# Twelve LayerNorm normalisations moved from VectorE to GpSimd in a linear-attention and ternary-FFN layer

## What is computed

```
xn  = (x - mean(x)) / sqrt(var(x) + 1e-5)          # over the last axis
q, k, v = xn @ Wq.T, xn @ Wk.T, xn @ Wv.T          # 16 heads, 16 features, 64 values
A   = tril(taylor_exp(q) @ taylor_exp(k).T)        # 1, x, x*x terms
y   = A @ v;  y = y * rsqrt(mean(y*y) + 1e-5) * g
f   = gelu(xn @ ternary(W1).T + b1) @ ternary(W2).T + b2
out = x + y @ Wo.T + f
```

## Time and profile before

| | us |
|---|---|
| median of 3 runs | 760.08 (760.06 to 760.13) |
| the profiled execution's own time | 760.95 |
| its span, slowest core (core 5) | 759.2 |
| spans of the other cores | 753.8 to 756.6 |
| PE, DVE, ACT, POOL busy | 691.8, 417.8, 243.4, 99.1 |
| mean granted TensorE clock, by core | 0.990 to 0.993 |

### The profile page before, as it was taken

One profiled execution on the slowest core, in us unless ns is written; L12 is line 12 of the kernel. 1 busy time (PEld: TensorE's weight loads), 2 busy tenths in 40 slices (PEclk: granted clock), 3 DMA queues, 4 the chain that ended last, 5 costly groups with the idle time before them and its releaser, 6 DMA issues.

```text
span 759.2 us, 11498 instructions; the slowest of 8 cores (753.8 to 759.2 us)
## 1 busy us (share of the span) xinstructions
PE 691.8 (91%) x4050; PEld 335.8 (44%) x4050; DVE 417.8 (55%) x623; ACT 243.4 (32%) x322; POOL 99.1 (13%) x131
## 2 busy tenths in 40 slices
PE   2777888877789888999999999999999999999998
PEld 1344544544445444444444444444444444444443
DVE  6667564678577566276556435351554554401653
ACT  3456666657557443222333333333100000000000
POOL 3112222224122211000000001010010000000000
PEclk9999999999999999999999999999999999999999
DMA  7974464766848624659786614533353676200883
GB/s 155 204 161 103 87 122 92 171 146 194 216 143 261 201 69 128 171 198 303 216 281 175 213 56 131 200 114 110 111 200 133 206 223 195 98 1 20 244 232 115
DMA packets 65415, 121.49 MB, mean 160 GB/s; under 512 B 22096, under 2 KB 28112, under 8 KB 65360
## 3 DMA queue, kind: packets, MB, share of 16 engines
q1 hardware_dynamic: 46752, 64.46, 28.0%
q0 software_dynamic: 18608, 56.30, 27.2%
HBM read 103.30 MB, written 16.78 MB: 158 GB/s over the span
## 4 chain that ended last, share of the span: by engine, by line
PE 81%; ACT 6%; DMA 5%; issue 4%; DVE 2%; POOL 2%; SPq 0%; ACTq 0%; DVEq 0%; POOLq 0%
PE pST L1199 8%; PE pY L1221 7%; PE pSS L1199 7%; PE pST L1221 7%; PE pW L1199 7%; PE pW L1221 7%; PE pSS L1221 7%; PE pY L1199 7%; PE pSS L977 4%; PE pW L1134 4%; PE pW L977 4%; PE pSS L1134 3%; ACT Am L922 3%; DMA xr<-x 2%; PE pSS L966 2%
## 5 line engine op out<-in xcount | busy, mean ns | idle before, releaser
L1221 PE MATMUL pY<-w2t,hT 128*128 128x512 bf16 x256 | 66.0, 379 | 0.1
L1221 PE MATMUL pST<-w2t,hT 128*128 128x512 bf16 x256 | 66.0, 379 | 0.0
L1221 PE MATMUL pSS<-w2t,hT 128*128 128x512 bf16 x256 | 66.0, 379 | 0.0
L1221 PE MATMUL pW<-w2t,hT 128*128 128x512 bf16 x256 | 66.0, 379 | 0.0
L524 POOL TENSOR_SCALAR_AFFINE_SELECT Am<-Am 128x1024 bf16<-128x1024 bf16 x32 | 35.3, 1104 | 208.4 <-ACT Am L922 208.4
L1199 PE MATMUL pST<-xnT,w1t 128*128 128x512 bf16 x272 | 61.5, 379 | 0.0
L1199 PE MATMUL pSS<-xnT,w1t 128*128 128x512 bf16 x256 | 57.9, 379 | 0.4 <-DVE consts L705 0.4
L1199 PE MATMUL pW<-xnT,w1t 128*128 128x512 bf16 x256 | 57.9, 379 | 0.0
L1199 PE MATMUL pY<-xnT,w1t 128*128 128x512 bf16 x240 | 54.2, 379 | 0.0
L719 DVE TENSOR_SCALAR w1t<-stg,consts 128x2048 bf16<-128x2048 f32 (+1 forms) x18 | 21.0, 1165 | 54.1 <-PE pY L1199 53.9
L517 POOL DMA_DIRECT2D stg<-w1r x32 | 25.1, 784 | 163.3 <-DVE w1t L722 147.5
(11 more groups left out here) (185 smaller groups left out, 1043.0 us busy)
## 6 DMA issues: line engine op xcount, KB each, us to landing
stg<-w1r POOLq DMA_DIRECT2D x32, 1024.0 KB, 7.5
stg<-w2r SPq DMA_DIRECT2D x16, 1024.0 KB, 9.0
stg<-w2r POOLq DMA_DIRECT2D x16, 1024.0 KB, 7.1
xr<-x SPq DMA_DIRECT2D x16, 512.0 KB, 5.2
res_scr<-rst SPq DMA_DIRECT2D x16, 512.0 KB, 3.2
res<-res_scr SPq DMA_DIRECT2D x32, 256.0 KB, 3.6
xs<-x SPq DMA_DIRECT2D x32, 256.0 KB, 3.9
out<-osb SPq DMA_DIRECT2D x32, 256.0 KB, 2.5
```

What stands on the lines that cost most here:

```text
L1221: return e.matmul(out_bank(n), hT[:, j, 128 * t:128 * t + 128], w2t[8 * dh + j // 4][:, j % 4, :], start=(j == 0), stop=(j == NJ - 1))
```

## The change

For tiles 4 to 15 the last step of LayerNorm, the subtraction and multiplication over 128x1024, is issued by GpSimd (`normalise`) in place of VectorE. VectorE keeps the statistics and the reciprocal (`ln_r`). In GpSimd's slot the late tile is normalised ahead of `affine_select`, and the slot's own tile behind it, ahead of the slot's DMA issues. VectorE gets two waits on `sXN`, ahead of bn_aggr and of the reciprocal, so that the statistics of tile t-2 aren't overwritten while GpSimd reads them. Tiles 0 to 3 stay as they were.

```diff
+        def normalise(t):
+            e.wait_ge(sLR, t + 1)
+            if t >= T_PE + 2:
+                unit_filled(e, ("t", t - 2))
+            e.tensor_scalar(xn_tm[:, t % 2, :], xr[:, t % 4, :],
+                            cc(C_MV + 2 * (t % 2)), cc(C_RC + t % 2),
+                            ALU.subtract, ALU.mult).then_inc(sXN, 1)
+
         for i in range(NI):
+            if i in LN_LATE:
+                normalise(LN_LATE[i])
 
             am = Am[:, i % 2, :, :]
             unit_emptied(e, ("s", i))
             e.affine_select(am, am, [[0, 8], [1, 128]], ALU.is_ge, 0.0, base=0,
                             channel_multiplier=-1).then_inc(gMK, 1)
+            if ln_tile(i) is not None:
+                normalise(ln_tile(i))
             if i < 2:
                 e.dma_start(out=wv[:, 1, 4 * i:4 * i + 4, :],
...
             e.wait_ge(sLB, 2 * t + 2)
+            if t >= T_PE + 2:
+                e.wait_ge(sXN, t - 1)
             e.bn_aggr(cc(C_MV + 2 * (t % 2), 2), cc(s6, 12)).then_inc(sLA, 1)
 
+        def ln_r(t):
+            e.wait_ge(sLS, t + 1)
+            if t >= T_PE + 2:
+                e.wait_ge(sXN, t - 1)
+            e.reciprocal(cc(C_RC + t % 2), cc(C_SD + t % 2)).then_inc(sLR, 1)
+
         def ln_b(t):
-            e.wait_ge(sLS, t + 1)
-            e.reciprocal(cc(C_RC + t % 2), cc(C_SD + t % 2)).then_inc(sLR, 1)
-            if t >= T_PE + 2:
-                unit_filled(e, ("t", t - 2))
-            elif t >= 2:
+            ln_r(t)
+            if t >= 2:
                 e.wait_ge(pT, t - 1)
...
             if i in LN_LATE:
-                ln_b(LN_LATE[i])
+                ln_r(LN_LATE[i])
...
             if ln_tile(i) is not None:
-                ln_b(ln_tile(i))
+                ln_r(ln_tile(i))
```

## The result

The changed kernel takes 774.64 us (median of 4 runs, 773.55 to 775.26), the kernel before beside it 760.11: ratio 1.0188, 95% interval 1.0176 to 1.0201, that is +14.3 us (13.4 to 15.3) on 760.11; the two medians differ by 14.5. Forecast was +2.8 us. The sign was right, the size five times too small, and the time lies outside the range. Some executions run longer whatever the kernel, with a lower granted clock on the cores of one die, and are left out of all ratios and medians here.

What follows compares the result with a forecast made beforehand. The chain lies on TensorE for 81% and VectorE for 2%, so relieving VectorE wins little. Terms -0.8 + 0.4 + 3.2 = +2.8 us on 760.08 give 762.9 us, range 760.9 to 765.6.

Steps and rivals of the forecast that it cites:

- The price of a tile on GpSimd: All twelve moved tiles: one normalisation on GpSimd takes 1.1 us, with 2.2 us as upper bound.
- Slot 3, query DMAs: Slot 3: four query DMAs wait behind tile 9's normalisation, so slot 4's scores move from 64.65 to 68.4, +3.8 us.
- Slots 1, 2 and 8, turning: Slots' own tiles: VectorE's next instruction waits for ScalarE anyway, so no gain; no cost was put on TensorE's turning.
- Slot 0, held products: Slot 0: GpSimd's mask, now later, holds VectorE's products of `features_k(0)`; +0.4 us, bounds 0 and +1.4.
- Slot 2, VectorE's gain: Slot 2: without the late tile, VectorE starts tile 8's statistics earlier and ScalarE's root follows; -0.8 us, bounds -0.8 and 0.
- rival (b): About the same time: a shorter wait ahead of slot 2's projection keeps the clock full; half gives +1.2, 761.3 us; chance 0.10.
- Slot 4: Slot 4 gives some back, with `own(5)` at 3.1 us: +3.2 us for slots 3 and 4 together, bounds +2.0 and +3.9.
- The late tiles: Tiles normalised ahead of the mask: the later mask costs nothing in slot 0, and 0 in slot 2, by 0.3 us.
- (a): Slower: a GpSimd tile takes 2.2 us, delaying query DMAs and slot 0 further; +4.9, 765.0 us; chance 0.15.
- (c): Faster: tile 9's reciprocal comes early enough that query DMAs land before slot 4's scores need them; -2.5, 757.6 us; chance 0.05.
- (d): VectorE's time moves, but eleven of twelve times into idle time; part of the forecast, no chance of its own.

Runs made afterwards that it cites:

- the cast run: Changed kernel with GpSimd's normalisation of the twelve tiles replaced by a copy into bf16, without subtraction and scaling: ratio 1.0033 to the kernel before, +2.5 us.
- the statistics first: Kernel before, all tiles on VectorE, with slot 2's statistics of tile 8 taken ahead of the normalisation of tile 7: 757.44 us, ratio 0.9970.

## Why the prediction was wrong

- **The price of a tile on GpSimd: the step that failed.** The prediction took 1.1 us from the mask's row and twice that, 2.2, as the upper bound. It measured 3.78. The nearest row was of another instruction, and twice it was no bound. Without this price there is no miss: 1.04 us a tile give +2.5 us, where +2.8 was forecast. That the two agree so closely is luck in part, because two other terms were off and cancel in that run: slot 2 gained 2.3 us in place of 0.8, and the step into slot 4 grew by 5.0 where the prediction's times give 3.4.
- **The parts of the miss.** Of the 11.5 us between +2.8 and +14.3, 2.7 are the tile's price in slot 3's chain, 1.5 the DMAs behind it, 5.3 the turnings (steps into slots 2, 3 and 9), 0.8 the gain of slot 2 that didn't come. These make 10.3; slot 0 takes 0.5 off, and about 1.7 us are not located.
- **Slot 3, query DMAs.** The mechanism was right in each link, and is the largest part: +8.4 us for tile 9 alone. The term said +3.8 for the scores; they came 8.0 later. Of this shortfall 2.7 us are the tile's price. Another 1.5 lie between the first issue and the scores, 4.9 us (median of the eight cores) in place of 3.4, with a landing of 3.3 us in place of 1.7: that x loads start "at about the old times" was true, but the DMAs were moved into that very moment.
- **Slots 1, 2 and 8, turning.** The prediction costed these tiles at nothing because VectorE's next instruction was covered. TensorE's turning had only the tile's old end to go by; no bound was worked out for how late a tile may come. The kernel before has it (core 5), tiles 5, 6 and 14 and their turnings:

```profile
35.53 0.81 DVE L570 TENSOR_SCALAR xn_tm<-xr,consts 128x1024 bf16<-128x1024 f32 x1
36.95 0.61 PE L1010 MATMUL pSS<-ident,xn_tm 128*128 128x128 bf16 x8
...
43.00 0.81 DVE L570 TENSOR_SCALAR xn_tm<-xr,consts 128x1024 bf16<-128x1024 f32 x1
44.09 0.61 PE L1010 MATMUL pSS<-ident,xn_tm 128*128 128x128 bf16 x8
...
103.23 0.81 DVE L570 TENSOR_SCALAR xn_tm<-xr,consts 128x1024 bf16<-128x1024 f32 x1
105.28 0.61 PE L1010 MATMUL pSS<-ident,xn_tm 128*128 128x128 bf16 x8
```

The turnings start 0.6, 0.3 and 1.2 us behind the tile's end, all without idle time. A tile that takes 3.0 us longer must come too late for them. The tile of 1.04 us takes 0.2 longer, and the steps into slots 2 and 9 are at +0.0 and +0.2; with 3.78 they are +2.7 and +1.1.

- **Slot 0, held products.** Forecast +0.4 with the 1.1 us tile, and the cast run has it: into slot 1 9.2 us, 8.8 before, one product 0.77 us in place of 0.23. In the changed kernel it is absent, since the mask comes after these products. There it meets the first product of the next set instead (0.53 us in place of 0.21 on four cores), and the step into slot 1 doesn't grow.
- **Slot 2, VectorE's gain.** -0.8 was right as a mechanism, and rival (b)'s clock came with it where the tile was cheap: -2.3 in the cast run, -2.5 with the statistics first, of which the order gives 0.9. In the changed kernel both drown in the wait for tile 6.
- **Slot 4.** That some of the wait is given back was right, and its size too: -0.6 from +3.8 to +3.2, and -0.5 to -0.6 measured. Two errors cancel in it. The squared scores start 1.11 us after the scores with ScalarE idle, not 0.7, so nothing is given back there; `own(5)` starts 0.3 earlier behind them. And `own(5)`, put at 3.1 us, took 2.3 (median; 3.2 and 3.4 on two cores, one of them the slowest), less than the 2.6 before.
- **The late tiles.** Costed at 0 for the mask; the run with the three back on VectorE agrees, even at 3.78 us.
- **Rivals.** (a) named the failed term, and its own price stopped at 2.2 us, 765.0 us. (b) is right as a mechanism; it shows in the cast run and with the statistics first, and never came to bear in the changed kernel (by its own numbers half of it gives +1.35, not +1.2). (c) fell: the scores of slot 4 were released by GpSimd's DMAs. (d) came true: nothing in the changed kernel's steps was won by VectorE's 9.6 us.

## What to carry to other kernels

Price an instruction on GpSimd by a row of that very instruction; if the trace has none, the nearest row isn't a bound; here it was off by 3.4 times. Of a queue into which work is put, look first for what is issued behind it and is wanted soon: one tile of 3.78 us ahead of four 16 KB DMAs cost more than the other eleven together. Then look for each reader of the result, how far behind the old end it starts: a tile that TensorE took up 0.3 us later had no room. And when a step releases two transfers at once, the large one can stand in front of the small ones that are waited for.

An engine can be relieved more cheaply by an exchange in its own queue: the statistics ahead of the normalisation in one slot gave 2.3 us (0.8 to 3.7), with nothing moved to another engine.

## What the runs showed of the hardware

The mask on GpSimd holds VectorE's two-input bf16 products, a tensor_scalar on GpSimd doesn't. In the cast run a product that starts 0.39 us behind the mask's start ends 0.07 behind its end, at 32.13 (0.77 us, not 0.23). In the changed kernel the products ran inside GpSimd's tile of 28.64 to 32.42 at their usual times:

```profile
28.64 3.78 POOL L524 TENSOR_SCALAR xn_tm<-xr,consts 128x1024 bf16<-128x1024 f32 x1 [15.31 <-DVE consts L580]
...
30.39 0.23 DVE L667 TENSOR_TENSOR kf<-vk 128x128 bf16<-128x128 bf16 x1 [1.93 <-ACT vk L881]
30.53 0.35 DVE L668 TENSOR_TENSOR kf<-vk 128x384 bf16<-128x384 bf16 x1
```

The Trainium skill (SBUF — State Buffer, SBUF: two separate sides) has the shared port pair held for the whole of a GpSimd operation, against VectorE operations with two SBUF inputs too. The runs bear that out for the mask; for the tensor_scalar they don't, and why isn't settled here.
